# Second-layer input codes of a bit-linear MLP: transposed by DMA from ScalarE's queue instead of by TensorE

## What is computed

```python
def bit_linear(x, w, b):
    gamma_x = clip(max(abs(x), axis=-1, keepdims=True), 1e-05, None)
    scale_x = 127.0 / gamma_x
    x_dq = clip(round(x * scale_x), -128.0, 127.0) / scale_x
    gamma_w = clip(mean(abs(w)), 1e-05, None)
    w_dq = clip(round(w / gamma_w), -1.0, 1.0) * gamma_w
    return einsum('bsd,hd->bsh', x_dq, w_dq) + b

def ffn(x):                      # D_MODEL = 512, HIDDEN = 2048
    gate = silu(bit_linear(x, gate_w, gate_b))
    val = bit_linear(x, val_w, val_b)
    return bit_linear(gate * val, out_w, out_b)

x = x + tanh(g_xattn) * xattn(layernorm(x), ctx, mask)
x = x + tanh(g_ffn) * ffn(layernorm(x))
```

## Time and profile before

| | us |
|---|---|
| median of 3 runs | 839.89 (839.85 to 842.77) |
| the profiled execution | 841.52 |
| its span, first to last instruction | 839.7 |

### The profile page before, as it was taken

The page is one execution under the profiler, slowest core; times in us unless marked ns, Lnnn a source line. Parts: engine busy times, 40 slices in busy tenths (PEclk is TensorE's granted clock), DMA queues, the critical chain, the costliest instruction groups (busy, mean ns, idle before and its releaser), DMA issues.

```text
span 839.7 us, 14590 instructions
## 1 busy us (share of the span) xinstructions
PE 750.2 (89%) x4886; PEld 384.6 (46%) x4886; DVE 697.7 (83%) x1412; ACT 534.0 (64%) x693; POOL 240.2 (29%) x427
## 2 busy tenths in 40 slices
PE   4695658969999999999999999999999999999995
PEld 4442344434544454445444544454445444454442
DVE  6778876898889888888988988988888888779982
ACT  4447858767557755784578557855676556745563
POOL 4101003221333324232433333314422332223431
PEclk9898768999999999999999999999999999999998
DMA  8572345101030103011211121111111020001000
GB/s 275 192 261 64 130 165 170 26 14 39 2 95 10 42 26 77 17 37 37 56 37 37 37 52 42 37 37 42 51 37 37 17 52 26 26 2 51 13 26 26
DMA packets 51663, 50.90 MB, mean 61 GB/s; under 512 B 30877, under 2 KB 30877, under 8 KB 50857
## 3 DMA queue, kind: packets, MB, share of 16 engines
q1 hardware_dynamic: 51624, 50.42, 19.2%
HBM read 39.91 MB, written 10.50 MB: 60 GB/s over the span
## 4 chain that ended last, share of the span: by engine, by line
PE 45%; DVE 31%; issue 11%; ACT 10%; POOL 1%; DMA 1%; DVEq 0%; POOLq 0%; ACTq 0%
PE psum L1444 14%; PE psum L1399 13%; PE psum L1435 7%; DVE arena L988 4%; DVE psum L983 3%; ACT arena L749 2%; DVE arena L1088 2%; PE psum L1402 2%; PE psum L1427 2%; PE psum L1378 2%; DVE xmax L1060 1%; DVE arena L1096 1%; PE psum L1470 1%; DVE stats L1048 1%; DVE arena L922 1%
## 5 line engine op out<-in xcount | busy, mean ns | idle before, releaser
L1399 PE MATMUL psum<-ternary,xqT 128*128 128x512 f16 x1024 | 261.3, 379 | 2.8 <-DVE xqT L1009 2.6
L554 POOL TENSOR_TENSOR rstd<-var_e,minus_half 128x1 f32<-128x1 f32 x64 | 40.0, 625 | 406.5 <-DVE var_e L1028 263.9
L1399 PEld LDWEIGHTS psum<-ternary,xqT 128*128 128x128 f16 x1024 | 96.3, 98 | 108.3 <-DVE xqT L1009 3.5
L1435 PE MATMUL psum<-ternary,arena 128*128 128x512 f16 x512 | 128.0, 383 | 1.2 <-ACT arena L726 1.2
L693 ACT ACTIVATE arena<-psum,dequant 128x512 f32<-128x512 f32 x128 | 87.2, 682 | 43.2 <-PE psum L1402 42.8
L983 DVE SCALAR_TENSOR_TENSOR psum<-psum,dequant,valb_b 128x512 f32<-128x512 f32 x128 | 96.3, 752 | 20.2 <-PE psum L1399 19.7
L988 DVE TENSOR_TENSOR arena<-psum,arena 128x512 f32<-128x512 f32 x128 | 88.5, 692 | 20.8 <-ACT arena L693 17.1
L1444 PE MATMUL psum<-wo_hi,arena 128*128 128x512 f16 x256 | 84.4, 392 | 2.5 <-DVE arena L1096 1.9
L1444 PE MATMUL psum<-arena,wq_hi 128*128 128x512 f16 x256 | 77.5, 385 | 7.1 <-ACT arena L740 7.1
L726 ACT ACTIVATE arena<-psum,round_c 128x1024 f16<-128x1024 f16 x64 | 71.3, 1114 | 19.1 <-PE psum L1427 18.7
L701 ACT ACTIVATE arena<-arena,round_c,hscale 128x1024 f32<-128x1024 f32 x64 | 75.9, 1236 | 4.6 <-DVE hscale L1004 4.4
(11 more groups left out here) (181 smaller groups left out, 1348.7 us busy)
## 6 DMA issues: line engine op xcount, KB each, us to landing
arena<-in_x SPq DMA_DIRECT2D x64, 256.0 KB, 2.7
out<-arena SPq DMA_DIRECT2D x32, 256.0 KB, 2.0
arena<-in_L_ffn_gate_w SPq DMA_DIRECT2D x4, 1024.0 KB, 10.0
arena<-in_L_ffn_out_w SPq DMA_DIRECT2D x3, 1024.0 KB, 9.6
ternary<-in_L_ffn_val_w SPq DMA_DIRECT2D x2, 1024.0 KB, 10.2
kcur<-k_scratch SPq DMA_DIRECT2D x64, 32.0 KB, 2.2
ternary<-in_ctx SPq DMA_DIRECT2D x1, 1024.0 KB, 5.4
ternary<-in_L_xattn_Wk SPq DMA_DIRECT2D x1, 1024.0 KB, 8.0
```

Source lines behind the costliest of these rows:

```text
L1399: ins = M.matmul(ps[:], xqT[:, t % 2, k, :], w[:, k, cols], start=(k == 0), stop=(w is wv and k == KC - 1))
L1435: ins = M.matmul(psO[:], hidT[:, k, :], wo2[:, k, :], start=(k == 0), stop=(k == FC - 1))
```

## The change

The codes of the second layer's input no longer go through TensorE and PSUM. ScalarE converts each half of the rounded `gs` to float16 codes in a buffer `hid16` in SBUF (`gs` less the constant `ROUND`, from a new column of `round_c`), waits until that is written, and issues a transposing DMA on its own queue. It goes from `hid16` into `hidT`, now two buffers, one for even and one for odd t. `down` waits for the DMA's semaphore. TensorE's `hidden_transpose` and ScalarE's `hidden_T` are gone. The new step stands on ScalarE after silu 0 and silu 1 (`CODES_AT = 0`), where `hidden_T` stood after silu 1 and silu 2. The wait for the earlier output block's eviction (`ys_ready`) moves from `hidden_transpose` to `down`.

```diff
-        hidT = room(2)[:, 0:2 * D].bitcast(F16).rearrange("p (k n) -> p k n", k=FC)
+        hidT = [r.bitcast(F16).rearrange("p (k n) -> p k n", k=FC) for r in (room(2)[:, 0:2 * D], room(3)[:, 2 * D:])]
+        hid16 = room(2)[:, 2 * D:].bitcast(F16)
...
                 def silu(t, n):
 
-                    if n == 0:
-                        last, u = ahead(b, t, -2)
-                        wait(act, hid_tr, last, 2 * u + 2)
...
-                def hidden_T(row, t, h):
-                    wait(act, hid_tr, row, 2 * t + h + 1)
-                    A.activation(hidT[:, h * FC // 2:(h + 1) * FC // 2, :].rearrange("p k n -> p (k n)"),
-                                 half(psO), ACT.Identity, bias=round_c[:, 1:2]).then_inc(hidT_ready.sem, 1)
+                def hidden_codes(row, t, h):
+
+                    cols = slice(h * F // 2, (h + 1) * F // 2)
+                    if h == 0:
+                        last, u = ahead(row, t, -1)
+                        wait(act, hidT_loaded, last, 16 * 2 * (u + 1))
+                    if ffn and not prev and (t, h) == (0, 0):
+                        act.wait_ge(s_wtr, 2 * W_GROUPS + 4)
+                    wait(act, hq_ready, row, 2 * t + h + 1)
+                    A.activation(hid16[:, cols], gs[:, t % 2, cols], ACT.Identity,
+                                 bias=round_c[:, 2:3]).then_inc(h16_ready.sem, 1)
+                    wait_alone(act, s_met_act, h16_ready, row, 2 * t + h + 1)
+                    act.dma_start_transpose(hidT[t % 2][:, h * FC // 2:(h + 1) * FC // 2, :],
+                                            hid16[:, cols]).then_inc(hidT_loaded.sem, 16)
...
-                        if down and n in (1, 2):
-                            hidden_T(*last, n - 1)
+                        if down and n in (CODES_AT, CODES_AT + 1):
+                            hidden_codes(*last, n - CODES_AT)
...
-                def hidden_transpose(row, t, h):
...
-                    for i in range(FC // 2):
-                        k = h * FC // 2 + i
-                        ins = M.transpose(half(psO)[:, i * P:(i + 1) * P], codes[:, k * P:(k + 1) * P], eye16[:])
-                    ins.then_inc(hid_tr.sem, 1)
-
                 def down(row, t, chunks):
 
                     if 0 in chunks:
-                        wait(pe, hidT_ready, row, 2 * t + 2)
+                        last, u = ahead(row, t, -1)
+                        wait(pe, ys_ready, last, u + 1)
+                        wait(pe, hidT_loaded, row, 16 * 2 * (t + 1))
...
-                        ins = M.matmul(psO[:], hidT[:, k, :], wo2[:, k, :], start=(k == 0), stop=(k == FC - 1))
+                        ins = M.matmul(psO[:], hidT[t % 2][:, k, :], wo2[:, k, :], start=(k == 0), stop=(k == FC - 1))
...
-                        if finish and i in (1, 2):
-                            hidden_transpose(*last, i - 1)
...
+CODES_AT = 0
```

More of the change, by code:

```diff
@@ L212, in build @@
         deq = sb("deq", [P, 3])
-        round_c = sb("round_c", [P, 2])
+        round_c = sb("round_c", [P, 3])
         minus_half = sb("minus_half", [P, 1])
@@ L274, in build @@
         s_wcopy = sem("weight_copied")
-        s_met_sp, s_met_dve, s_met_pool = (sem(f"{e}_waits_met") for e in ("sync", "vector", "pool"))
+        s_met_sp, s_met_dve, s_met_pool, s_met_act = (sem(f"{e}_waits_met") for e in ("sync", "vector", "pool", "scalar"))
         s_amax1 = sem("largest_of_partitions")
@@ L337, in build @@
         hq_ready = per_row("hidden_rounded", NT * 2)
-        hid_tr = per_row("hidden_transposed", NT * 2)
-        hidT_ready = per_row("hidT_ready", NT * 2)
+        h16_ready = per_row("hidden_codes_ready", NT * 2)
+        hidT_loaded = per_row("hidT_loaded", 16 * NT * 2)
         o_done = per_row("out_product", NT)
@@ L892, in _ @@
             V.memset(round_c[:, 0:1], ROUND)
+            V.memset(round_c[:, 2:3], -ROUND)
             then(V.memset(round_c[:, 1:2], -HALF))
@@ L1414, in xq_transpose, with down @@
                              start=True, stop=True).then_inc(xq_tr.sem, 1)
-                def hidden_transpose(row, t, h):
-                    codes = low(gs[:, t % 2, :])
-                    wait(pe, hq_ready, row, 2 * t + h + 1)
-                    if h == 0:
+                def down(row, t, chunks):
+                    if 0 in chunks:
                         last, u = ahead(row, t, -1)
                         wait(pe, ys_ready, last, u + 1)
-                    else:
-                        wait(pe, hidT_ready, row, 2 * t + 1)
-                    for i in range(FC // 2):
-                        k = h * FC // 2 + i
-                        ins = M.transpose(half(psO)[:, i * P:(i + 1) * P], codes[:, k * P:(k + 1) * P], eye16[:])
-                    ins.then_inc(hid_tr.sem, 1)
-                def down(row, t, chunks):
-                    if 0 in chunks:
-                        wait(pe, hidT_ready, row, 2 * t + 2)
+                        wait(pe, hidT_loaded, row, 16 * 2 * (t + 1))
                     for k in chunks:
-                        ins = M.matmul(psO[:], hidT[:, k, :], wo2[:, k, :], start=(k == 0), stop=(k == FC - 1))
+                        ins = M.matmul(psO[:], hidT[t % 2][:, k, :], wo2[:, k, :], start=(k == 0), stop=(k == FC - 1))
                     if FC - 1 in chunks:
```

## The result

| | us |
|---|---|
| the changed kernel, median of 4 runs | 867.87 (863.96 to 869.68) |
| the kernel before, on the same chip, median of 4 | 840.32 (839.85 to 842.77) |
| ratio | 1.032, 95% interval 1.027 to 1.036 |
| span of the profiled execution | 866.6, before 839.7 |

A forecast was written before the change was run, and what follows sets the result against it. The prediction took TensorE as the bound (busy 82.84 of 85.7 us a row), VectorE close behind. It added 27 us in seven rows, 10 in the last and 5 at the end: +42, giving 882 us, range 826 to 960.

The follow-up runs named there:

- e2_issue_only: The changed kernel with the DMAs still issued on ScalarE, but the output product reads the untransposed codes and waits only for the conversion; 861.7 us.
- e6_again: The changed kernel with SyncE issuing the transposing DMAs, ahead of the key loads and the store; a later run of the same kernel; 832.52 us.
- e7_codes_later: The changed kernel with the codes step behind silu 1 and silu 2 instead of silu 0 and silu 1; 937.53 us.

## What to carry over

Before a DMA is put on the queue of an engine that also computes, price its issue as work of that engine, with the short wait for its own operand, and ask at each place who stands behind it, on the other engines too: a block in which the bounding engine loses nothing can hand its delay to the next. An engine that only issues DMAs is the better place, if the new transfer goes ahead of those that wait for later events; here this turned 3.2% slower into 1% faster. At the end of the program, where no other work covers a landing, the path through TensorE and ScalarE was the shorter one (5.8 against 8.1 us).

## What the runs showed of the hardware

- A transposing DMA from SBUF to SBUF took 1.25 us of ScalarE's queue for eight blocks of 128x128 float16 and 1.24 us of SyncE's, 1.30 us for four blocks, and for sixteen 1.33 us at least and 1.82 in the median; a plain load of 256 KB took 0.33 us. It landed after 2.6, 3.1 and 4.5 us for four, eight and sixteen blocks.
- The 64 transposing DMAs were 67584 packets for 16.79 MB, 248 bytes each on the mean. With them on ScalarE's queue the residual x landed after 3.5 us instead of 2.7, also in `e2_issue_only`. The bytes alone don't do it: it was 2.8 us with the same DMAs on SyncE's queue (`e6_again`) and with the step one silu later (`e7_codes_later`).

```profile
q10 hardware_dynamic: 67584, 16.79, 10.5%
...
arena<-in_x SPq DMA_DIRECT2D x64, 256.0 KB, 3.5
```

- In t = 1 of the loop rows, waits of TensorE of 1.8, 2.2 and 1.8 us were followed by a stretch at the lower clock (0.55 granted on the mean from 460.2 to 463.6), waits of 2.1 and 2.5 us were not.
